# A graph layer and an FFN on one core: the first two FFN units spread over the last two neighbour sums, and ten bias adds moved behind the adjacency

## The chip, the cores and the metric

One core of a Trainium2 chip. The metric is the device time of one execution in microseconds; the median of three runs of the kernel before is 371.93. The engines are named as in the profile: PE is TensorE's matmuls and PEld its weight loads, DVE is VectorE, ACT is ScalarE, POOL is GpSimd, SP is SyncE, which issues the DMAs.

## The reference

x has 1250 nodes (rows) of 512 features; src and dst are 20000 edges, sorted by dst.

```python
def _L0_gnn_ref(x, src, dst, W_self, W_neigh, b):
    msg_sum = jax.ops.segment_sum(x[src], dst, num_segments=N_NODES)
    deg = jax.ops.segment_sum(jnp.ones((src.shape[0],), x.dtype), dst, num_segments=N_NODES)
    neigh = msg_sum / jnp.maximum(deg, 1.0)[:, None]
    h = x @ W_self + neigh @ W_neigh + b
    h = jnp.where(h >= 0, h, LEAKY_SLOPE * h)
    norm = jnp.sqrt(jnp.sum(h * h, axis=1, keepdims=True))
    return h / jnp.maximum(norm, EPS)
def _quantize_weight(w, group_size):
    o, i = w.shape
    wg = w.reshape(o, i // group_size, group_size)
    scale = jnp.mean(jnp.abs(wg), axis=-1, keepdims=True) + EPS
    wq = jnp.clip(jnp.round(wg / scale), -1.0, 1.0) * scale
    return wq.reshape(o, i)
...
gate = _bitlinear(x, w_gate)
up = _bitlinear(x, w_up)
h = jax.nn.silu(gate) * up
return _bitlinear(h, w_down)
...
x = x + _L0_gnn_ref(_layernorm(x, axis=-1), src, dst, L0_gnn_W_self, L0_gnn_W_neigh, L0_gnn_b)
x = x + _L0_ffn_ref(_layernorm(x, axis=-1)[None], L0_ffn_w_gate, L0_ffn_w_up, L0_ffn_w_down)[0]
```

The FFN is 512 to 1408 and back; a group of the quantiser is 128 inputs, so each 128x128 block of a weight is a ternary block (-1, 0, 1) times one scale for each of its output rows.

## The kernel before, in words

The kernel is written engine by engine. Each engine runs its list of instructions in order; semaphores tie the lists together, and an instruction that waits holds up all that is behind it on its engine. Nodes come in ten tiles of 125 (t = 0 to 9), features in four blocks of 128.

**First stage.** 80 slots, eight for each tile. In them TensorE multiplies tile t's normalised rows with W_neigh (y, kept as a high and a low part, `y_hi` and `y_lo`) and with W_self (z), and in between builds the adjacency `a_t` from one-hot rows: VectorE makes `hot_dst` (L904) and `hot_src` (L900), ScalarE copies finished blocks of 40 nodes out (`block_out`, L682). Beside that the 34 weight loads of the FFN are made ternary, a load being up to four 128x128 blocks: ScalarE takes absolute values and their sums (`abs_of`, L642), GpSimd makes of a load's sums a threshold `thr` (L561) and the scales `nscale` (L562), and VectorE compares (`ternary_of`, L841), which waits for both. Two loads can be in ScalarE's absolute values at a time, four in `raw`. 25 loads are done in this stage, and nine of the down weights (33 blocks; called load 0 to 8 here) later. GpSimd also adds the bias to each z tile, in the slots:

```python
for slot in range(SLOTS + 8):
    t, i = divmod(slot, 8)
    for j in jobs_in(slot, 7):
        ... scales_of(l)
    if i == 4 and 1 <= t <= NT:
        ...
        pool.wait_ge(z_out, t)
        nc.gpsimd.tensor_tensor(z[:, t - 1, :], z[:, t - 1, :], bias_b[0:TP, :], ALU.add).then_inc(z_done, 1)
for l in range(LOADS1, len(loads)):
    scales_of(l)
```

**Neighbour sums.** Sum n (n = 0 to 9) is 20 matmuls on TensorE (L1127) into banks 4 and 5 in turn. Then, for tile n: VectorE `neighbour_sum` (L925, from PSUM into z), `leak` (L931), ScalarE square and root (L727, L729), VectorE `residual` (L937 to L948: x_sb and its layer-norm statistics), ScalarE's root (L691), VectorE `shift1` (L953, L955), ScalarE `normalize1` (L697, into one of two buffers `xn`), TensorE's transpose (L1039), ScalarE `x1_high` (L704) and VectorE `x1_low` (L960). Sum n+2 waits for `neighbour_sum(n)`. In program order the steps of tiles trail: `residual(n - 1)` in turn n of VectorE, `normalize1(n - 2)` on ScalarE, the transpose of tile n-3 after sum n on TensorE. The ternary blocks of loads 0 to 8 are spread over turns 1 to 6.

**FFN.** 33 units (f, c): f is one of 11 blocks of 128 of the 1408, c one of three groups of tiles (0 to 2, 3 to 5, 6 to 9; 378, 378 and 504 columns). A unit has eight gate and up pieces (G0, U0, G1, ... U3), each two matmuls into one of seven banks; ScalarE takes G0 and U0 out of PSUM (L748), VectorE the other six (L997), accumulating with the scale of the block. Then ScalarE's SiLU (L770), GpSimd h = silu times up (L595), ScalarE `h_hi` (L787), GpSimd `h_lo` (L604). Three units later come four down pieces D1, D2, D3, D0; ScalarE takes D1 and D3 into `d_one` and GpSimd adds them to `acc` (L585), VectorE takes the others. Ternary blocks go through bank 7: transposed on TensorE (L1110, L1114), out with a sign on ScalarE (L714, L717). Units 0 to 5 are (0,0), (0,1), (1,0), (1,1), (0,2), (1,2). When a tile group is complete, output pieces (O) transpose `acc` (L1174), and the tile is added to x_sb by VectorE (L1031), or by ScalarE and GpSimd (L802, L612), and stored. A turn n of the FFN is the gate and up pieces of unit n with the down pieces of unit n-3.

## Time and profile before

| | |
|---|---|
| median of 3 runs | 371.93 us (371.62 to 371.94) |
| the profiled execution | 372.08 us, its span 370.1 us |
| PE busy | 340.7 us, 92% of the span |
| DVE busy | 312.9 us, 85% |
| ACT busy | 235.4 us, 64% |
| POOL busy | 173.8 us, 47% |
| mean granted TensorE clock | 0.989 |

How to read it: TensorE is the busiest engine, but a share of the whole span hides that the stages differ. The busy time of TensorE is modelled from the ends of pipelined matmuls; the distance between the starts of two matmuls tells more than their durations. In the timelines the first number is the start in us from the span's start, the second the us that it lasted, and brackets at the end hold how long the engine was idle before, and who released it.

### The profile page before, as it was taken

The page shows a single profiled execution, that of the slowest core. Times are in us where ns is not written, and L with a number is a line of the kernel's source. Part 1 is how long each engine was busy: PE and PEld are TensorE (multiplying, and loading weights), DVE is VectorE, ACT ScalarE, POOL GpSimd, SP SyncE. Part 2 cuts the span into 40 slices and gives each one's busy share as a digit, 9 for nine tenths or more (in the row PEclk, how much of TensorE's full clock was granted, in tenths as well). Part 3 has the DMA queues.
Part 4 walks back from the last instruction along what each step waited for, and adds up shares of the span by engine and source line. Part 5 has one row for each costly group of instructions (what it writes and reads, how often), then busy time and mean ns, then how long its engine had stood idle before and what let it go on. Part 6 is the DMA issues. An engine that isn't in the chain of part 4 may idle for free.

```text
span 370.1 us, 5903 instructions
## 1 busy us (share of the span) xinstructions
PE 340.7 (92%) x1741; PEld 260.3 (70%) x1741; DVE 312.9 (85%) x746; ACT 235.4 (64%) x637; POOL 173.8 (47%) x218
## 2 busy tenths in 40 slices
PE   2988999999999999999866999999999999999992
PEld 1444555555555667778655888889899898889981
DVE  2599999898898517999688799999999988999994
ACT  2174877777768224775556777777676678776660
POOL 3003343342122210111003456788788887799990
PEclk9999999999999999999989999999999999999997
DMA  7951222322212101200000000000000000000214
GB/s 229 291 143 45 71 83 60 86 58 70 74 50 81 31 1 30 75 25 0 3 0 2 0 1 2 0 3 1 0 3 0 2 2 2 0 0 3 90 34 156
DMA packets 9412, 16.70 MB, mean 45 GB/s; under 512 B 1062, under 2 KB 1886, under 8 KB 9378
## 3 DMA queue, kind: packets, MB, share of 16 engines
q1 hardware_dynamic: 9300, 16.21, 15.4%
q8 instruction: 15, 0.25, 0.3%
q14 instruction: 19, 0.16, 0.1%
q10 hardware_dynamic: 78, 0.08, 0.1%
HBM read 13.73 MB, written 2.56 MB: 44 GB/s over the span
## 4 chain that ended last, share of the span: by engine, by line
PE 63%; DVE 23%; ACT 7%; POOL 3%; issue 2%; POOLq 0%; DVEq 0%; ACTq 0%
PE bank L1198 39%; PE bank L1087 9%; PE bank L1127 5%; DVE hot_dst L904 4%; DVE tq_gu L841 3%; PE bank L1048 3%; DVE tq_d L841 2%; ACT mag_early L642 2%; PE bank L464 2%; DVE bn L946 2%; DVE x_sb L943 1%; DVE bn L827 1%; PE bank L1039 1%; DVE z L925 1%; DVE hot_src L900 1%
## 5 line engine op out<-in xcount | busy, mean ns | idle before, releaser
L1198 PE MATMUL bank<-x_hi,t_gu 128*128 128x378 f32 (+1 forms) x264 | 96.2, 364 | 3.6 <-DVE x_lo L960 2.8
L1198 PE MATMUL bank<-x_lo,t_gu 128*128 128x378 f32 (+1 forms) x264 | 94.7, 359 | 0.0
L1087 PE MATMUL bank<-w_sb,xnT 128*125 128x512 f32 x160 | 87.6, 635 | 2.2 <-ACT z L672 1.5
L997 DVE SCALAR_TENSOR_TENSOR g_acc<-bank,nscale,g_acc 128x378 f32<-128x378 f32 (+1 forms) x99 | 64.3, 650 | 11.9 <-PE bank L1198 11.3
L561 POOL TENSOR_SCALAR thr<-absum 128x4 f32<-128x4 f32 (+1 forms) x34 | 15.8, 464 | 112.2 <-ACT mag_early L642 79.5
L997 DVE SCALAR_TENSOR_TENSOR u_acc<-bank,nscale,u_acc 128x378 f32<-128x378 f32 (+1 forms) x99 | 64.1, 647 | 0.6 <-PE bank L1198 0.6
L595 POOL TENSOR_TENSOR hh<-sg,u_acc 128x378 f32<-128x378 f32 (+1 forms) x32 | 35.1, 1097 | 57.6 <-ACT sg L770 57.4
L1048 PEld LDWEIGHTS bank<-hot_dst,hot_src 128*125 128x125 bf16 x281 | 32.2, 137 | 39.9 <-issue 22.2
L585 POOL TENSOR_TENSOR acc<-acc,d_one 128x378 f32<-128x378 f32 (+1 forms) x57 | 60.1, 1055 | 0.0
L1198 PEld LDWEIGHTS bank<-x_hi,t_gu 128*128 128x128 f32 x264 | 50.4, 191 | 8.1 <-DVE x_lo L960 3.5
L1198 PEld LDWEIGHTS bank<-x_lo,t_gu 128*128 128x128 f32 x264 | 50.6, 192 | 3.6
L904 DVE TENSOR_SCALAR hot_dst<-iota,key 128x400 bf16<-128x400 uint16 x157 | 47.4, 340 | 4.7 <-PE bank L1048 4.3
L1198 PE MATMUL bank<-h_hi,t_d 128*128 128x378 f32 (+1 forms) x132 | 48.1, 364 | 0.0
L1198 PE MATMUL bank<-h_lo,t_d 128*128 128x378 f32 (+1 forms) x132 | 46.6, 353 | 0.0
L642 ACT ACTIVATE mag_early<-raw 128x128 f32<-128x128 f32 x99 | 29.6, 301 | 23.9 <-DVE tq_gu L841 22.3
L1048 PE MATMUL bank<-hot_dst,hot_src 128*125 128x240 bf16 (+4 forms) x281 | 40.4, 264 | 3.0 <-DVE hot_dst L904 3.0
L997 DVE SCALAR_TENSOR_TENSOR acc<-bank,nscale,acc 128x378 f32<-128x378 f32 (+1 forms) x63 | 40.1, 645 | 1.0 <-POOL acc L585 1.0
L1127 PE MATMUL bank<-y_hi,a_t 125*125 125x512 f32 x100 | 40.1, 401 | 0.0
L1127 PE MATMUL bank<-y_lo,a_t 125*125 125x512 f32 x100 | 39.5, 395 | 0.0
L604 POOL TENSOR_TENSOR h_lo<-hh,h_hi 128x378 fp32r<-128x378 f32 (+1 forms) x32 | 35.0, 1095 | 3.4 <-ACT h_hi L787 1.9
L748 ACT ACTIVATE d_one<-bank,nscale 128x378 f32<-128x378 f32 (+1 forms) x57 | 34.8, 610 | 2.1 <-PE bank L1198 1.9
L748 ACT ACTIVATE g_acc<-bank,nscale 128x378 f32<-128x378 f32 (+1 forms) x33 | 20.2, 612 | 24.3 <-PE bank L1198 24.3
(107 smaller groups left out, 549.4 us busy)
## 6 DMA issues: line engine op xcount, KB each, us to landing
raw<-in_L_ffn_w_gate SPq DMA_DIRECT2D x11, 256.0 KB, 2.7
raw<-in_L_ffn_w_up SPq DMA_DIRECT2D x11, 256.0 KB, 2.6
out_x<-x_sb SPq DMA_DIRECT2D x10, 224.0 KB
raw<-in_L_ffn_w_down SPq DMA_DIRECT2D x8, 256.0 KB, 2.6
x_sb<-in_x SPq DMA_DIRECT2D x1, 1344.0 KB
w_sb<-in_L_gnn_W_neigh SPq DMA_DIRECT2D x1, 1024.0 KB, 6.2
w_sb<-in_L_gnn_W_self SPq DMA_DIRECT2D x1, 1024.0 KB, 7.1
raw<-in_L_ffn_w_down SPq DMA_DIRECT2D x4, 192.0 KB, 2.3
```

Source lines behind the costliest of these rows:

```text
L585: nc.gpsimd.tensor_tensor(to, to, d_one[:, o, slot, 0:width(u)], ALU.add).then_inc(d_added, 1)
L595: nc.gpsimd.tensor_tensor(hh[:, u % 2, 0:w], sg[:, u % 2, 0:w], u_acc[:, u % 2, 0:w], ALU.mult).then_inc(h_done, 1)
L604: nc.gpsimd.tensor_tensor(h_lo[:, u % h_slots, 0:w], hh[:, u % 2, 0:w], h_hi[:, u % h_slots, 0:w].bitcast(F32), ALU.subtract).then_inc(hlo ...
L642: nc.scalar.activation(mag_of(j), raw_of(j), ACT.Abs, accum_out=absum[:, j:j + 1]).then_inc(abs_done, 1)
L748: nc.scalar.activation(to, bank_of(u, what)[:, 0:width(u)], ACT.Copy, scale=nscale[:, j:j + 1]).then_inc(act_took, 1)
L841: nc.vector.scalar_tensor_tensor(out=tq_of(j), in0=mag_of(j), scalar=thr[:, j:j + 1], in1=raw_of(j), op0=ALU.is_gt, op1=ALU.mult).then_inc ...
L904: nc.vector.tensor_scalar(hot_dst[:, c % HOT, :], iota[:, 0:NT * WIN], key[:, c:c + 1], None, ALU.is_equal).then_inc(hot_made, 1)
L997: nc.vector.scalar_tensor_tensor(out=to, in0=bank_of(u, what)[:, 0:w], scalar=nscale[:, j:j + 1], in1=to, op0=ALU.mult, op1=ALU.add).then_ ...
L1048: last = nc.tensor.matmul(bank[k % 3][0:TP, 0:NT * WIN].rearrange("p (s d) -> p s d", d=WIN)[:, :, d0:d0 + n], hot_src[:, c // SB % SBS, c ...
L1087: last = nc.tensor.matmul(to[0:TP, :], xnT[:, t, k * TP:(k + 1) * TP], w_sb[:, k, half * D:(half + 1) * D], start=k == 0, stop=k == KD - 1)
L1127: last = nc.tensor.matmul(bank[4 + n % 2][0:TP, :], a_t[:, s, n * TP:(n + 1) * TP], y[:, s, :], start=s == 0 and y is y_hi, stop=s == NT - ...
L1198: last = nc.tensor.matmul(to, w, parts[h], start=h == 0, stop=h == 1)
```

## The change

Units 1 and 2 change places. The pieces of units 0 and 1 are issued between the matmuls of sums 8 and 9 (`EARLY_AT`: one piece after each of the steps 1 to 8 of a sum), over banks 2 and 6. The nine late loads are done in VectorE's turns up to 3 (`DOWN`). A tile's steps trail its sum by less: residual in its own turn, the transpose after sum t+2. GpSimd's bias adds come after `block_out`, and one instruction makes all scales at the end. The down pieces of units 0 and 1 come in turn 5, those of 2 and 3 in turn 6, and the order is as before from turn 7 on. g_acc and u_acc have four buffers, h has five slots, and the FFN's buffers lie at other addresses. D3 of unit 31 goes to ScalarE and GpSimd, and the outputs of tiles 0 to 2 come one turn later.

```diff
-    h_slots = 4
+    h_slots = 5
+        DOWN = [0, 3, 5, 7, 8, NL]
         def down_jobs(n):
-            lo, hi = (LOADS1 + max(0, min(NL, 3 * i // 2)) for i in (n, n + 1))
+            lo, hi = (LOADS1 + DOWN[min(max(i, 0), len(DOWN) - 1)] for i in (n + 1, n + 2))
-        UNITS = [(0, 0), (0, 1), (1, 0), (1, 1), (0, 2), (1, 2)]
+        UNITS = [(0, 0), (1, 0), (0, 1), (1, 1), (0, 2), (1, 2)]
-            return what in ("G0", "U0") or what in ("D1", "D3")[:max(0, min(2, NU - 1 - u))]
+            return what in ("G0", "U0") or what in ("D1", "D3")[:2 if u < NU - 1 else 0]
+        EARLY = 2
+        EARLY_AT = [1, 2, 3, 4, 5, 6, 7, 8]
+            downs[{0: 5, 1: 5, 2: 6, 3: 6}.get(u, u + LAG)].append(u)
-                if n == (u + LAG + 1 if u < NU - 3 else NU + LAG - 1):
+                if n == {FINAL[0]: FINAL[0] + LAG + 1, FINAL[1]: NU + LAG - 2, FINAL[2]: NU + LAG - 1}[u]:
-        RING = [2, 6, 1, 0, 4, 3, 5]
+        RING = [2, 6] * (4 * EARLY) + [2, 6, 4, 5, 3] * 4
+        RING += [[2, 6, 4, 5, 3, 0, 1][i % 7] for i in range(len(pieces) - len(RING))]
...
# GpSimd
+            for l in range(LOADS1):
                 scales_of(l)
+            pool.wait_ge(bias_in, 16)
+            pool.wait_ge(block_out, NB)
+            for t in range(NT):
+                pool.wait_ge(z_out, t + 1)
+                nc.gpsimd.tensor_tensor(z[:, t, :], z[:, t, :], bias_b[0:TP, :], ALU.add).then_inc(z_done, 1)
+                if 1 <= t <= NL:
+                    scales_of(LOADS1 + t - 1)
+
+            nc.gpsimd.tensor_scalar(nscale[:], absum[:], 1.0 / P, Q_EPS, ALU.mult, ALU.add).then_inc(nscales, 1)
...
# VectorE
+            for j in down_jobs(-1):
+                ternary_of(j)
+            for n in range(NT):
+                neighbour_sum(n)
+                leak(n)
+                if n >= 1:
+                    shift1(n - 1)
+                if n >= 2:
+                    x1_low(n - 2)
+                u = n - NT + 3
+                if u >= 0:
+                    take(u, "G1")
+                    if u < EARLY:
+                        take(u, "U1")
+                residual(n)
+                if 0 <= u < EARLY:
+                    for what in ("G2", "U2", "G3", "U3"):
+                        take(u, what)
+                for j in down_jobs(n):
+                    ternary_of(j)
...
# TensorE
+                    if s == NT - 1:
+                        last.then_inc(n_ready, 1)
+                    if u >= 0 and s in EARLY_AT:
+                        piece(8 * u + EARLY_AT.index(s))
...
+                if n >= 2:
+                    transpose_x1(n - 2)
```

GpSimd's list from the last load of the first stage to down load 1 (thr is the threshold, z the bias add), before:

```order
L561 TENSOR_SCALAR thr<-absum 128x4 [waits abs_done]
L562 TENSOR_SCALAR nscale<-absum 128x4
L574 TENSOR_TENSOR z<-z,bias_b 125x512 [waits z_out] x2
L561 TENSOR_SCALAR thr<-absum 128x4 [waits abs_done]
L562 TENSOR_SCALAR nscale<-absum 128x4
L561 TENSOR_SCALAR thr<-absum 128x3 [waits abs_done]
L562 TENSOR_SCALAR nscale<-absum 128x3
```

and with the change:

```order
L590 TENSOR_SCALAR thr<-absum 128x4 [waits abs_done]
L598 TENSOR_TENSOR z<-z,bias_b 125x512 [waits z_out,block_out,bias_in]
L598 TENSOR_TENSOR z<-z,bias_b 125x512 [waits z_out]
L590 TENSOR_SCALAR thr<-absum 128x4 [waits abs_done]
L598 TENSOR_TENSOR z<-z,bias_b 125x512 [waits z_out]
L590 TENSOR_SCALAR thr<-absum 128x3 [waits abs_done]
L598 TENSOR_TENSOR z<-z,bias_b 125x512 [waits z_out]
```

All ten adds have moved behind the last adjacency block, and from the third on each stands between two thresholds.

VectorE's list from the degrees to sum 1 (tq_d is a ternary block, z from a bank the sum, z from z the leak), before:

```order
L916 RECIPROCAL rdeg<-rs 125x6 [waits rdeg_done]
L925 SCALAR_TENSOR_TENSOR z<-bank,rdeg,z 125x512 [waits z_done,n_ready,rdeg_done]
L931 SCALAR_TENSOR_TENSOR z<-z 125x512 [waits hsum]
L925 SCALAR_TENSOR_TENSOR z<-bank,rdeg,z 125x512 [waits z_done,n_ready]
L937 TENSOR_SCALAR nrm<-nrm 125x1 [waits norms]
```

and with the change:

```order
L959 RECIPROCAL rdeg<-rs 125x6 [waits rdeg_done]
L884 SCALAR_TENSOR_TENSOR tq_d<-mag_late,thr,raw 128x128 [waits scales,rdeg_done]
L884 SCALAR_TENSOR_TENSOR tq_d<-mag_late,thr,raw 128x128 [waits scales] x10
L968 SCALAR_TENSOR_TENSOR z<-bank,rdeg,z 125x512 [waits z_done,n_ready]
L974 SCALAR_TENSOR_TENSOR z<-z 125x512 [waits hsum]
L980 TENSOR_SCALAR nrm<-nrm 125x1 [waits norms]
L982 RECIPROCAL inv<-nrm 125x1 [waits inv_done]
L984 SCALAR_TENSOR_TENSOR x_sb<-z,inv,x_sb 125x512 [waits inv_done]
L987 BN_STATS bn<-x_sb 125x6 [waits x1_done]
L989 BN_AGGR mv_118<-bn 125x2 [waits bn_done]
L884 SCALAR_TENSOR_TENSOR tq_d<-mag_late,thr,raw 128x128 [waits scales] x8
L968 SCALAR_TENSOR_TENSOR z<-bank,rdeg,z 125x512 [waits z_done,n_ready]
```

Eleven ternary blocks now stand ahead of sum 0 and eight ahead of sum 1, and the residual of tile 0 is in its own turn.

ScalarE's list from the first SiLU to unit 4's first take (sg is the SiLU, g_acc from a bank a take; only unit 4 has 504 columns here), before:

```order
L770 ACT_TABLE_LOAD
L770 ACTIVATE sg<-g_acc 128x378
L787 ACTIVATE h_hi<-hh 128x378
L714 ACTIVATE t_gu<-bank 128x1024
L704 ACTIVATE x_hi<-bank 128x504
L748 ACTIVATE g_acc<-bank,nscale 128x378
L748 ACTIVATE u_acc<-bank,nscale 128x378
...
L717 ACTIVATE t_d<-bank 128x512
L748 ACTIVATE g_acc<-bank,nscale 128x504
```

and with the change:

```order
L731 ACTIVATE x_hi<-bank 128x504
L800 ACT_TABLE_LOAD
L800 ACTIVATE sg_78<-g_acc_70 128x378
L800 ACTIVATE sg_79<-g_acc_71 128x378
L806 ACTIVATE h_hi<-hh_80 128x378
L806 ACTIVATE h_hi<-hh_81 128x378
L800 ACTIVATE sg_78<-g_acc_72 128x378
L746 ACTIVATE t_d_90<-bank 128x512
L806 ACTIVATE h_hi<-hh_80 128x378
L762 ACTIVATE g_acc_70<-bank,nscale 128x504
```

The SiLU and h_hi steps of units 0 to 2, which stood between takes, now stand together behind the last tile's x_hi and ahead of unit 4's first take.

## Rows read from the trace of the kernel before

**Rows 1.** Windows: stretch, us, busy PE, PEld, DVE, ACT, POOL (count), clock, DMA share, GB/s.
```profile
185.00:195.00 10.00, 6.18 (x29) 5.47 (x30) 8.63 (x21) 5.57 (x12) 0.00 (x0) 0.83 0.00 0
195.00:205.00 10.00, 6.39 (x45) 5.45 (x43) 7.64 (x15) 6.32 (x11) 3.94 (x4) 1.00 0.01 2
215.00:300.00 85.00, 85.00 (x487) 76.97 (x486) 79.51 (x139) 61.94 (x115) 68.44 (x66) 1.00 0.01 1
```

**Rows 2.** Waits of TensorE from 10 to 127 us.
```profile
PE bank L1087 <- ACT z L672: 1.5, 4, 0.6
```

**Rows 3.** Timeline of TensorE: start us, us, line, operation [idle before <-releaser].
```profile
155.57 0.65 PE L1039 MATMUL bank<-ident,xn 126*128 126x126 f32 x4 [0.73 <-ACT xn L697]
166.24 0.48 PE L1127 MATMUL bank<-y_hi,a_t 125*125 125x512 f32 x1
171.31 0.47 PE L1127 MATMUL bank<-y_hi,a_t 125*125 125x512 f32 x1
182.02 0.40 PE L1127 MATMUL bank<-y_lo,a_t 125*125 125x512 f32 x1
204.74 0.42 PE L1198 MATMUL bank<-x_hi,t_gu 128*128 128x378 f32 x1
224.73 0.34 PE L1198 MATMUL bank<-x_hi,t_gu 128*128 128x378 f32 x1
```

**Rows 4.** Chain that ended last: start us, us, what.
```profile
188.00 3.48 PE bank L1198 x10
204.98 3.84 PE bank L1198 x22
```

**Rows 5.** Timelines of GpSimd and VectorE near 43 us.
```profile
43.00 1.27 POOL L574 TENSOR_TENSOR z<-z,bias_b 125x512 f32<-125x512 f32 x1
43.08 1.61 DVE L841 SCALAR_TENSOR_TENSOR tq_gu<-mag_early,thr,raw 128x128 bf16<-128x128 f32 x2
46.05 0.60 DVE L841 SCALAR_TENSOR_TENSOR tq_gu<-mag_early,thr,raw 128x128 bf16<-128x128 f32 x2
```

**Rows 6.** Timelines of ScalarE and VectorE in the sums.
```profile
127.58 0.65 ACT L682 ACTIVATE a_t<-bank 125x400 fp32r<-125x400 f32 x2 [1.67 <-PE bank L1048]
132.59 0.75 DVE L925 SCALAR_TENSOR_TENSOR z<-bank,rdeg,z 125x512 f32<-125x512 f32 x1 [5.66 <-PE bank L1127]
134.86 0.20 ACT L729 ACTIVATE nrm<-ss 125x1 f32<-125x1 f32 x1
139.42 0.75 DVE L925 SCALAR_TENSOR_TENSOR z<-bank,rdeg,z 125x512 f32<-125x512 f32 x1 [5.35 <-PE bank L1127]
154.17 1.13 DVE L841 SCALAR_TENSOR_TENSOR tq_d<-mag_late,thr,raw 128x128 bf16<-128x128 f32 x4
155.22 0.74 DVE L925 SCALAR_TENSOR_TENSOR z<-bank,rdeg,z 125x512 f32<-125x512 f32 x1
192.03 0.14 DVE L937 TENSOR_SCALAR nrm<-nrm 125x1 f32<-125x1 f32 x1
193.92 0.18 DVE L948 BATCH_NORM_AGGREGATE mv<-bn 125x2 f32<-125x6 f32 x1
```

**Rows 7.** Timelines of ScalarE and GpSimd at the first SiLU.
```profile
194.45 1.28 ACT L770 ACT_TABLE_LOAD   x1
196.35 0.99 POOL L595 TENSOR_TENSOR hh<-sg,u_acc 128x378 f32<-128x378 f32 x1 [27.50 <-ACT sg L770]
197.97 0.98 POOL L604 TENSOR_TENSOR h_lo<-hh,h_hi 128x378 fp32r<-128x378 f32 x1 [0.63 <-ACT h_hi L787]
```

**Rows 8.** Timelines of VectorE, GpSimd, TensorE in the tail.
```profile
357.74 0.60 DVE L997 SCALAR_TENSOR_TENSOR acc<-bank,nscale,acc 128x378 f32<-128x378 f32 x1
358.39 2.55 POOL L612 TENSOR_TENSOR x_sb<-x_sb,d_one 125x512 f32<-125x512 f32 x2
361.85 2.17 DVE L997 SCALAR_TENSOR_TENSOR acc<-bank,nscale,acc 128x378 f32<-128x378 f32 x4 [0.98 <-POOL acc L585]
364.17 1.76 PE L1174 MATMUL bank<-ident,acc 128*125 128x128 f32 x12 [2.90 <-DVE acc L997]
```

More of the change, by code:

```diff
@@ L403, in bank_of @@
         def bank_of(u, what):
-            return bank[RING[index[u, what] % len(RING)]]
+            return bank[RING[index[u, what]]]
         def nodes_of(u):
@@ new lines, in _, with silu, high_of_h @@
+            ternary_out(0, 1)
+            normalize1(NT - 1)
+            take(3, "G0", g_of(3))
+            take(3, "U0", u_of(3))
+            x1_high(NT - 1)
+            def silu(u):
+                act.wait_ge(dve_took, took[u, "G3"])
+                if u >= 2:
+                    act.wait_ge(h_done, u - 1)
+                nc.scalar.activation(sg_of(u), g_of(u), ACT.Silu).then_inc(silu_done, 1)
+            def high_of_h(u):
+                act.wait_ge(h_done, u + 1)
+                if u >= h_slots:
+                    act.wait_ge(piece_ready, index[u - h_slots, "D0"] + 1)
+                nc.scalar.activation(h_hi[:, u % h_slots, 0:width(u)], hh_of(u), ACT.Copy).then_inc(hhi_done, 1)
@@ L771, in _ @@
                 for what in ("D1", "D2", "D3"):
-                    v = n - LAG
-                    if 0 <= v and by_act(v, what):
-                        o = int(what[1])
+                    for v in downs[n]:
+                        if not by_act(v, what):
+                            continue
                         if (v, what) not in added:
-                            take(v, what, acc[:, o, nodes_of(v)])
+                            take(v, what, acc[:, int(what[1]), nodes_of(v)])
@@ L1005, in low_of_h @@
                                         ALU.subtract).then_inc(hlo_done, 1)
-            for n in range(NU + LAG):
+            for n in range(EARLY, NU + LAG):
                 for what in TURN:
-                    u = n - LAG if what[0] == "D" else n
-                    if 0 <= u < NU and not by_act(u, what):
-                        take(u, what)
+                    for u in units_of(n, what):
+                        if not by_act(u, what) and (u, what) != (EARLY, "G1"):
+                            take(u, what)
+                    if n == 2 and what == "U1":
+                        shift1(NT - 1)
+                    if n == 2 and what == "U2":
+                        x1_low(NT - 2)
                     if n == 3 and what == "U1":
-                        x1_low(9)
+                        x1_low(NT - 1)
                     if n == NU - 1 and what == "U3":
@@ new lines, in transpose_x1, with output_piece @@
+            def transpose_x1(t):
+                if t >= 2:
+                    pe.wait_ge(xlo_done, t - 1)
+                transpose_xn(t, normed1, x1_bank(t), x1n_T, TQ)
+            def output_piece(t):
+                v = out_of[t]
+                pe.wait_ge(dve_took, took[v, "D0"])
+                for o in range(1, KD):
+                    if by_act(v, f"D{o}"):
+                        pe.wait_ge(d_added, added[v, f"D{o}"])
+                for k in range(KD):
+                    last = nc.tensor.transpose(bank_of(t, "O")[0:TP, k * P:(k + 1) * P], acc[:, k, t * TQ:t * TQ + TP], ident[:])
+                last.then_inc(piece_ready, 1)
@@ L1161, in _, with piece @@
+            def piece(i):
+                u, what = pieces[i]
+                if bank_before[i] is not None:
+                    old = pieces[bank_before[i]]
                     pe.wait_ge(took_sem(*old), took[old])
                 else:
[L1164 to L1165 removed]
+                    pe.wait_ge(*{2: (block_out, NB), 6: (z_out, NT), 4: (hsum, NT - 1), 5: (hsum, NT), 3: (squares, NT),
+                                 0: (xlo_done, NT - 1), 1: (xlo_done, NT)}[RING[i]])
@@ L1166, in _ @@
                 if what == "O":
-                    v = out_of[u]
-                    pe.wait_ge(dve_took, took[v, "D0"])
-                    for o in range(1, KD):
-                        if by_act(v, f"D{o}"):
-                            pe.wait_ge(d_added, added[v, f"D{o}"])
-                    for k in range(KD):
-                        last = nc.tensor.transpose(bank_of(u, what)[0:TP, k * P:(k + 1) * P], acc[:, k, u * TQ:u * TQ + TP], ident[:])
-                    last.then_inc(piece_ready, 1)
```

314 lines of the change are left out of this document (144 added, 170 removed).

## The prediction

> **What bounds the kernel now.** I read a table of stretches first, then the waits, the timeline of TensorE, and then the places where engines hand over to each other. The stretches [rows 1] show an FFN stage in which TensorE is busy all the time (85 of 85 us), and just ahead of it two poor stretches (6.2 and 6.4 us busy of 10, from 185 to 205 us). In the first stage (projections and adjacency, to 127.4 us) TensorE waits 1.5 us in all for ScalarE's z [rows 2]; its other wait there, for the first hot rows, the change does not touch. In the sums TensorE waits 0.73 us at 155.57 for a normalised tile; the last sum is out at 182.42, and the even run of FFN pieces starts at 204.74 [rows 3]. Of these 22.3 us the 48 matmuls of units 0 to 2 fill 8.4, at 3.84 us for 22 [rows 4], and the transposes 2.7, so it waits some 11. Part of it runs slow: ten matmuls take 3.48 us there, not 1.75 [rows 4], at a granted clock that averages 0.83 [rows 1], so partly at 1.2 GHz. From 204.74 on TensorE is the bound.
>
> **What the change moves.** (a) 32 matmuls (units 0 and 1) go from that gap into sums 8 and 9. (b) GpSimd's ten bias adds on z leave the first stage; they start when the last adjacency block is out, and alternate with the thresholds of the down weights. (c) All 33 down ternaries on VectorE stand in front of sum 4's work. (d) Tile t's transpose stands after sum t+2 on TensorE, was after t+3. (e) ScalarE's first SiLU steps stand behind tile 9 and ahead of unit 4's takes. (f) The output pieces of tiles 0 to 2 stand one turn later.
>
> **First stage: -1.0 us.** A bias add takes 1.27 us. One starts at 43.00, and the two ternaries that VectorE begins at 43.08 take 1.61 us together, where two take 0.60 otherwise [rows 5]. So such an add on GpSimd keeps an instruction of this kind off for about 1.0 us. With the change that leaves VectorE's first stage, but TensorE sees of it only the 1.5 us for ScalarE's z, whose queue holds absolute values that wait for VectorE's ternaries. Between 0 and 1.5 I take 1.0, since the lateness grows step by step behind these ternaries.
>
> **Early sums: +9.3 us.** This term decides. I keep the clock of the trace of before. The last block is out at 128.23 [rows 6]. GpSimd then adds bias 0 and 1 (to 130.8), makes threshold 0 (131.1) and at once starts bias 2: as at 43.00, the add is ahead of the ternary that waited for its scale. From then on each of the down loads 0 to 7 pays a hold of 1.0 us [rows 5], and four ternaries 1.05 (154.17 to 155.22 [rows 6]), three 0.8. Loads 0 to 2 come ahead of sum 0 on VectorE: with the thresholds, and ScalarE's absolute values of load 2 that can start only when load 0 is ternary, VectorE is free at 137.1; before, it took sum 0 up at 132.59.
> One turn of VectorE costs 4.5 us without ternaries: 2.45 from taking up a sum to ScalarE's root (132.59 to 135.06), and 2.1 for the residual and statistics (192.03 to 194.10) [rows 6]; the shift and x_lo of other tiles fit below ScalarE's part. So VectorE takes up sum 1 at 137.1 + 4.5 + 2 x 2.05 = 145.7, sum 2 at 145.7 + 4.5 + 1.8 + 2.05 = 154.05, sum 3 at 154.05 + 4.5 + 2.05 + 0.4 (degrees) = 161.0, and sum 4 at 161.0 + 4.5 + 0.8 = 166.3. Before, it took up sum 1 at 139.42 and sum 4 at 155.22 [rows 6].
> Tile t-1 is normalised 2.45 + 0.8 = 3.25 us after VectorE takes up sum t: tile 0 at 148.95, tile 1 at 157.3, tile 2 at 164.25. TensorE has ended sum 2 at 144.9 and stands, in order, at tile 0's transpose: a wait of 4.05. A sum and a transpose cost 5.07 (166.24 to 171.31 [rows 3]), 4.63 of it the sum. Sum 3 ends at 154.0, wait 3.3; sum 4 at 162.35, wait 1.9; sum 5 ends at 169.75, and tile 3 is there at 169.55. The waits sum to 9.25. Behind each waiting transpose stand all later sums; the waits in turn give VectorE time, so it is not late any more at sum 7.
> The bounds: with no hold at all the same chain gives waits of 0.15, 1.3 and 0.9, together 2.4; with a hold for the whole 1.27 it gives 11.4. I take the 1.0 of the row, which is the same pair of instructions.
>
> By the Trainium skill, "SBUF — State Buffer", section Who interferes with whom, VectorE and GpSimd have one pair of ports in common: a VectorE instruction with two SBUF inputs and a GpSimd instruction that reads SBUF exclude each other, and the later one waits for all of the other. The pair at 43.08 shows the exclusion, but 1.0 us of it. By the page the early sums would cost 11.4 us, and the sum below would be 380.9.
>
> **From sum 8 to unit 7: -0.7 us.** Without these waits sum 8 would start at 171.31 - 0.73 + 0.43 (one more transpose) + 1.1 (three weight transposes) = 172.1. Sums 8 and 9 hold eight pieces each (16 matmuls, 2.8 us) over only two banks. VectorE takes piece G2 behind the residual, so G3 gets its bank 7.05 us into the sum, not 5.8: sum 8 lasts 8.67, the transpose 0.43, sum 9 is out after 8.85, at 190.05. Call this R; before, R was 182.42 [rows 3].
> After R: root +2.5; residual and statistics behind one take +5.0; ScalarE's root +5.35; shift behind another take +5.8; tile 9 normalised +6.65. Its transpose stands behind piece U1 of unit 3, whose bank VectorE frees at +7.95, so x_hi of tile 9 is out at +9.7. Then table load and SiLU, 1.9 to GpSimd's h (194.45 to 196.35), and GpSimd and ScalarE hand over to each other: from h to h_lo 1.62, h_lo 0.98 [rows 7]. Unit 4's first take on ScalarE stands behind h_hi of unit 2, so this passes twice, 5.2, and then h, h_hi and the take of G0, 2.1. That is +18.9, and +19.1 with VectorE 0.2 late. TensorE has five pieces of unit 4 done at +12.8 and stands 6.3 us at the sixth for G0's bank. To unit 7 it is then the 20.0 us of before (204.74 to 224.73 [rows 3]) less unit 3 (2.8), its weight transpose (0.2) and five wide pieces (2.3), plus 0.2 of slow takes: 14.9. Unit 7 starts at 190.05 + 19.1 + 14.9 = 224.05, before at 224.73. The gap is not filled: most of it comes again behind other instructions.
>
> **Clock: +1.0 us.** Before, ten matmuls took 1.7 us too long after two waits of together 2.8 us [rows 4]. After one of 6.3 I expect the same; part of it lies under the takes. Bounds 0 and 1.7.
>
> **Tail: -1.9 us.** Before, two output adds on GpSimd (358.39 to 360.94) stand ahead of its last accumulation; VectorE waits 0.98 us for that at 361.85, and the last transposes start at 364.17 [rows 8]. Now the accumulations stand ahead, and one more of them is GpSimd's. VectorE: D0 of unit 30 ends at 358.3 [rows 8], two takes 359.3, an output add 360.0, four takes 362.1; transposes at 362.2. TensorE is through with its pieces near 360.1 (28 matmuls and transposes from 355.9) and covers none of it. Bounds 0 (the added accumulation of 1.0 ends last) and -2.4.
>
> **Sum.** The profiled execution took 372.08 us, 0.15 above the median of 371.93. 372.08 + 9.3 - 0.7 + 1.0 - 1.0 - 1.9 = 378.8. The layout, the single scale instruction and the fifth h slot I cost at nothing: GpSimd has nothing to do between the last threshold and unit 0's SiLU, which covers the 132-column scale; were it late, the first take in sum 8 would be late by as much, under 1 us.
>
> **Rivals.** *The holds cost nothing in the sums (chance 0.10).* For it: the same adds ran beside a full VectorE in the first stage, and TensorE lost next to nothing. Against: there the hot rows are made ahead; here TensorE waits in order for what VectorE makes. Waits of 2.4 instead of 9.3: 371.9.
> *TensorE never waits at the early transposes (0.22), faster.* For it: VectorE was idle 5.66 and 5.35 us before it took up sums 0 and 1 [rows 6], which would hold the 8.7 us of ternaries, if the adds fall in other gaps and ScalarE has its absolute values early. Against: the add comes right after the threshold each time. 378.8 - 9.3 = 369.5. It decides from 2.6 us of waits: with less than that the change wins.
> *The clock falls at each early wait too (0.13), slower.* Against: TensorE is ahead of VectorE there, so a slow sum is hidden. Three times 1.7 on top, less what is hidden: up to 383.5.
> *My forecast (0.55): 378.8*, its own range 376.5 to 381.5 (tail 0, clock 0 or 1.7, hold 1.27).
>
> **Numbers.** Range 369.0 to 382.5: it leaves out about half of the faster case and most of the slowest. 0.2% (0.74 us) is about what a measurement of this kernel can tell from no change. Slower 0.55 + 0.13 = 0.68; same 0.10; faster 0.22.
>
> **What would show it.** In the changed trace: down ternaries with maxima near 1.3 us between 131 and 160; TensorE idle for 3 to 4 us before the tile transposes after sums 2 and 3, released by ScalarE's xn; sum 8 starting near 180.4; an idle of 6 us some 13 us after the last sum, released by ScalarE's take; unit 7 near 232. I am wrong if GpSimd's adds are through before VectorE wants its thresholds, or if ScalarE's takes of unit 4 come before h of unit 2.

## The result and the profile after

The changed kernel takes 383.09 us (median of four executions, 382.71 to 384.0), the kernel before 371.94 beside it (371.62 to 372.07): 1.030 times as long, 95% interval 1.028 to 1.032. The forecast was 378.8 with a range to 382.5, so the direction was right and the size too small. The profiled execution took 382.97 us, of which the span is 380.9; before it was 372.08 and 370.1. Every comparison of places below is made inside these spans.

The waits of TensorE from 127 to 230 us, in the changed kernel (line, what it waited for, us in total, times, longest):

```profile
PE bank L1086 <- ACT xn L724: 10.2, 4, 4.9
PE bank L1218 <- ACT g_acc L762: 5.6, 1, 5.6
PE bank L1218 <- DVE g_acc L1023: 2.2, 2, 1.1
```

Its timeline of TensorE, as in [rows 3]; L1236 is a neighbour sum, L1086 a tile's transpose, L1218 a piece of the FFN, L1182 the last transposes:

```profile
125.75 0.51 PE L1236 MATMUL bank<-y_hi,a_t 125*125 125x512 f32 x1
...
148.40 1.10 PE L1086 MATMUL bank<-ident,xn 126*128 126x126 f32 x4 [4.91 <-ACT xn L724]
...
156.84 0.65 PE L1086 MATMUL bank<-ident,xn 126*128 126x126 f32 x4 [1.14 <-ACT xn L724]
...
164.19 0.62 PE L1086 MATMUL bank<-ident,xn 126*128 126x126 f32 x4 [2.07 <-ACT xn L724]
...
199.06 0.40 PE L1236 MATMUL bank<-y_lo,a_t 125*125 125x512 f32 x1
...
218.84 0.79 PE L1218 MATMUL bank<-x_hi,t_gu 128*128 128x504 f32 x1 [5.62 <-ACT g_acc L762]
219.43 0.62 PE L1218 MATMUL bank<-x_lo,t_gu 128*128 128x504 f32 x1
...
236.33 0.34 PE L1218 MATMUL bank<-x_hi,t_gu 128*128 128x378 f32 x1
...
373.95 1.55 PE L1182 MATMUL bank<-ident,acc 128*125 128x128 f32 x12 [1.64 <-DVE acc L1023]
```

Both groups of waits that were forecast are there: three at the early transposes, and one of 5.6 us before a piece of unit 4, which ends when ScalarE takes G0 out. Sum 9 ends at 199.3, so that one begins 13.9 us later. The table of stretches, with the columns of [rows 1] (PE and PEld busy, VectorE, ScalarE, GpSimd, then the granted clock), shows one thing that was priced too low:

```profile
127.00:155.00 28.00, 23.09 (x96) 17.11 (x95) 22.27 (x44) 11.61 (x64) 12.64 (x16) 0.88 0.15 43
...
205.00:215.00 10.00, 8.12 (x39) 6.24 (x37) 6.72 (x13) 5.40 (x9) 2.80 (x3) 0.88 0.00 0
215.00:225.00 10.00, 6.16 (x22) 4.93 (x23) 3.99 (x6) 5.18 (x10) 5.02 (x6) 0.66 0.00 0
```

From 215 to 225 us the granted clock averages 0.66, so most of that stretch ran at 1.2 GHz, and the wide matmuls from 218.84 on stand 0.42 us apart, where they stand 0.23 apart at the full clock.

The timeline of GpSimd where the down weights begin (POOL L598 is the bias add, L590 the threshold, DVE L884 the ternary, ACT L669 the absolute value):

```profile
126.69 2.56 POOL L598 TENSOR_TENSOR z<-z,bias_b 125x512 f32<-125x512 f32 x2 [12.46 <-issue]
129.33 0.20 POOL L590 TENSOR_SCALAR thr<-absum 128x4 f32<-128x4 f32 x1
129.61 1.30 POOL L598 TENSOR_TENSOR z<-z,bias_b 125x512 f32<-125x512 f32 x1
131.00 0.20 POOL L590 TENSOR_SCALAR thr<-absum 128x3 f32<-128x3 f32 x1
131.27 1.30 POOL L598 TENSOR_TENSOR z<-z,bias_b 125x512 f32<-125x512 f32 x1
```

The timeline of VectorE beside it (L968 takes up sum 0):

```profile
129.63 1.43 DVE L884 SCALAR_TENSOR_TENSOR tq_d<-mag_late,thr,raw 128x128 bf16<-128x128 f32 x1 [4.38 <-POOL thr L590]
131.25 1.47 DVE L884 SCALAR_TENSOR_TENSOR tq_d<-mag_late,thr,raw 128x128 bf16<-128x128 f32 x1
...
136.88 0.74 DVE L968 SCALAR_TENSOR_TENSOR z<-bank,rdeg,z 125x512 f32<-125x512 f32 x1
...
149.67 4.03 DVE L884 SCALAR_TENSOR_TENSOR tq_d<-mag_late,thr,raw 128x128 bf16<-128x128 f32 x7
158.27 2.28 DVE L884 SCALAR_TENSOR_TENSOR tq_d<-mag_late,thr,raw 128x128 bf16<-128x128 f32 x4
165.38 0.87 DVE L884 SCALAR_TENSOR_TENSOR tq_d<-mag_late,thr,raw 128x128 bf16<-128x128 f32 x3
```

And ScalarE's first absolute value of load 2:

```profile
133.07 0.31 ACT L669 ACTIVATE mag_late<-raw 128x128 f32<-128x128 f32 x1 [4.01 <-DVE tq_d L884]
```

A ternary takes 0.34 us, and three in a row 0.87 (165.38, where no add is left). The one that begins with the add at 129.61 ends 0.15 us behind it, after 1.43, and the one at 131.25 again ends 0.15 behind an add. By the Trainium skill, "SBUF — State Buffer", section Who interferes with whom, the later of two such instructions waits for all of the other. The trace agrees that it does not end before the other is through; the loss is 1.1 us (1.43 less 0.34) beside an add of 1.30. The 1.0 us that I took from [rows 5] was a little short for one pair, not for the mean over all loads.

In the first stage, TensorE's waits for ScalarE's z fall from the 1.5 us of [rows 2] to 0.8. Its first matmul on hot rows, the kernel before above the changed one:

```profile
21.62 0.85 PE L1048 MATMUL bank<-hot_dst,hot_src 128*125 128x240 bf16 x3 [1.36 <-DVE hot_dst L904]
```

```profile
21.16 0.85 PE L1095 MATMUL bank<-hot_dst,hot_src 128*125 128x240 bf16 x3 [1.36 <-DVE hot_dst L947]
```

From there to the start of sum 0 it is 105.81 us before (to 127.43) and 104.59 with the change (to 125.75).

### The profile page after: what moved, and what is told of

It reads as the page before. It is cut to its first block, busy times and chain, and to the rows that moved or that the text cites. A ratio compares the mean times of both kernels' runs of the same rounds, so it can differ in the third digit from the quotient of the medians.

```text
span 380.9 us, 5900 instructions
## 1 busy us (share of the span) xinstructions
PE 344.7 (90%) x1741; PEld 263.6 (69%) x1741; DVE 316.1 (83%) x745; ACT 236.3 (62%) x638; POOL 160.4 (42%) x186
## 4 chain that ended last, share of the span: by engine, by line
PE 67%; DVE 17%; issue 6%; ACT 5%; POOL 3%; DVEq 0%; ACTq 0%; POOLq 0%
PE bank L1218 37%; PE bank L1134 13%; PE bank L1236 5%; PE bank L1095 4%; DVE tq_d L884 4%; DVE hot_dst L947 2%; PE bank L1086 2%; PE bank L1157 1%; DVE bn L870 1%; DVE tq_gu L884 1%; PE bank L1182 1%; ACT bank L753 1%; DVE z L968 1%; DVE z L974 1%; DVE acc L1023 1%
## 5 line engine op out<-in xcount | busy, mean ns | idle before, releaser
L1218 PE MATMUL bank<-x_hi,t_gu 128*128 128x378 f32 (+1 forms) x264 | 97.4, 369 | 7.9 <-ACT g_acc L762 5.6
L1218 PE MATMUL bank<-x_lo,t_gu 128*128 128x378 f32 (+1 forms) x264 | 96.0, 364 | 0.0
L590 POOL TENSOR_SCALAR thr<-absum 128x4 f32<-128x4 f32 (+1 forms) x34 | 11.2, 329 | 123.9 <-ACT mag_early L669 100.6
L1218 PEld LDWEIGHTS bank<-x_hi,t_gu 128*128 128x128 f32 x264 | 51.1, 194 | 14.8 <-ACT g_acc L762 6.1
L611 POOL TENSOR_TENSOR acc<-acc,d_one 128x378 f32<-128x378 f32 (+1 forms) x58 | 61.1, 1057 | 0.0
L947 DVE TENSOR_SCALAR hot_dst<-iota,key 128x400 bf16<-128x400 uint16 x157 | 44.6, 319 | 11.8 <-PE bank L1095 11.2
L1218 PEld LDWEIGHTS bank<-x_lo,t_gu 128*128 128x128 f32 x264 | 51.1, 194 | 4.3
L1218 PE MATMUL bank<-h_hi,t_d 128*128 128x378 f32 (+1 forms) x132 | 48.5, 368 | 0.2
L1218 PE MATMUL bank<-h_lo,t_d 128*128 128x378 f32 (+1 forms) x132 | 46.7, 354 | 0.0
L669 ACT ACTIVATE mag_early<-raw 128x128 f32<-128x128 f32 x99 | 29.6, 301 | 21.0 <-DVE tq_gu L884 19.8
L1236 PE MATMUL bank<-y_hi,a_t 125*125 125x512 f32 x100 | 41.3, 413 | 0.0
L1236 PE MATMUL bank<-y_lo,a_t 125*125 125x512 f32 x100 | 40.4, 404 | 0.0
L762 ACT ACTIVATE g_acc<-bank,nscale 128x378 f32<-128x378 f32 (+1 forms) x33 | 20.2, 613 | 30.7 <-PE bank L1218 30.6
```

Source lines behind the costliest of these rows:

```text
L611: nc.gpsimd.tensor_tensor(to, to, d_one[o][slot][:, 0:width(u)], ALU.add).then_inc(d_added, 1)
L669: nc.scalar.activation(mag_of(j), raw_of(j), ACT.Abs, accum_out=absum[:, j:j + 1]).then_inc(abs_done, 1)
L762: nc.scalar.activation(to, bank_of(u, what)[:, 0:width(u)], ACT.Copy, scale=nscale[:, j:j + 1]).then_inc(act_took, 1)
L947: nc.vector.tensor_scalar(hot_dst[:, c % HOT, :], iota[:, 0:NT * WIN], key[:, c:c + 1], None, ALU.is_equal).then_inc(hot_made, 1)
L1218: last = nc.tensor.matmul(to, w, parts[h], start=h == 0, stop=h == 1)
L1236: last = nc.tensor.matmul(bank[4 + n % 2][0:TP, :], a_t[:, s, n * TP:(n + 1) * TP], y[:, s, :], start=s == 0 and y is y_hi, stop=s == NT - ...
```

## The experiments

The profiled executions begin their sums at 124.8 to 127.4 us, also where the first stage is the same. So I compare places by the time since the first matmul of sum 0. The scatter lies ahead of the first matmul on hot rows, which starts between 20.2 and 21.8 us; these are the rows that the adjacency is built from. From there to sum 0 it is 105.8 us in the kernel before and e4, 104.9 in e1, e3, e6, e7 and e9, and 104.6 in the changed kernel, e2, e5, e8, e10 and e11, each time within 0.03 us. All medians are on a chip beside the kernel before (372.0 in each of the three sets of experiments). "Ladder" names the fuller reorder of ScalarE's list in e5.

| kernel | median us | sum 0 starts | sum 8, after sum 0 | end of sum 9 | last transposes | end, after those |
|---|---|---|---|---|---|---|
| before | 371.94 | 127.43 | 43.88 | 54.6 | 236.74 | 5.93 |
| changed | 383.09 | 125.75 | 55.29 | 73.3 | 248.20 | 6.95 |
| e1 adds back | 373.98 | 126.72 | 46.38 | 64.4 | 238.38 | 6.80 |
| e2 takes ahead | 379.81 | 125.39 | 55.28 | 73.3 | 245.55 | 6.86 |
| e3 both | 371.17 | 125.41 | 46.41 | 64.4 | 235.10 | 7.99 |
| e4 tail alone | 370.67 | 126.90 | 43.88 | 54.6 | 234.84 | 6.76 |
| e5 ladder | 375.81 | 126.34 | 55.28 | 73.3 | 241.14 | 6.92 |
| e6 ladder, adds back | 366.73 | 125.93 | 46.41 | 64.4 | 231.68 | 7.99 |
| e7 as e6, O turn | 368.12 | 126.25 | 46.36 | 64.4 | 233.60 | 5.95 |
| e8 adds moved alone | 374.14 | 125.57 | 47.19 | 58.0 | 240.81 | 6.02 |
| e9 as e6, spread | 369.24 | 125.65 | 46.89 | 64.9 | 232.72 | 6.83 |
| e10 half adds | 375.26 | 124.77 | 49.65 | 67.7 | 241.23 | 6.80 |
| e11 spread, adds moved | 381.03 | 125.95 | 54.59 | 72.6 | 246.03 | 6.72 |

(Places from the timelines of TensorE; the end of sum 9 is the start of its last matmul, the last column the span less the start of the last transposes.)

**e1: the bias adds back in the first stage.**

```diff
-            for l in range(LOADS1):
-                scales_of(l)
-            pool.wait_ge(bias_in, 16)
-            pool.wait_ge(block_out, NB)
-            for t in range(NT):
-                ... add bias to tile t, scales_of(LOADS1 + t - 1)
+            for slot in range(SLOTS + 8):
+                ... scales of the slot's jobs; add bias to tile t - 1 if i == 4
+            for l in range(LOADS1, len(loads)):
+                scales_of(l)
```

> The changed kernel with GpSimd's ten bias adds back in the slots of the first stage, as in the kernel before; the ternaries in front, the transposes two sums behind and the rest stay. Theory 1 (the early sums are late because each bias add keeps one down ternary of VectorE off for 1.1 to 1.2 us): no ternary after 127 us lasts over 0.4 us, the first sum starts 1.7 us later (127.4, was 125.75), the waits before the transposes after sums 2, 3 and 4 (8.1 us) and the slow sum 3 (2.2 us) shrink to 0 to 2.4 us, sum 8 starts at 172 to 174.5 (was 181.05), and the time is 374 to 377. Theory 2 (the order does it: eight ternaries and more ahead of sum 0's work, and transposes one sum earlier than before, adds or no adds): the waits stay at 6 us or more and the time stays at 380 or above, or gets worse by the 1.7 us of the first stage.

Measured: 373.98 us, ratio to before 1.004 (1.001 to 1.006), 9.1 less than the changed kernel. The ternaries after 127 us in one row (min, median, max in ns):

```profile
L888 DVE SCALAR_TENSOR_TENSOR tq_d<-mag_late,thr,raw x33: 321/347/354, 129.8 to 158.0; 128x128 bf16<-128x128 f32 x33
```

And in TensorE's timeline the waits that are left, before the transposes after sums 3 and 4:

```profile
150.04 0.65 PE L1090 MATMUL bank<-ident,xn 126*128 126x126 f32 x4 [0.51 <-ACT xn L728]
156.25 0.62 PE L1090 MATMUL bank<-ident,xn 126*128 126x126 f32 x4 [0.93 <-ACT xn L728]
```

No ternary is long, and sum 8 comes 8.9 us earlier after sum 0. Theory 1 holds. Its 1.7 us for the first stage was wrong: from the first hot rows to sum 0 the adds cost 0.3 us here (104.92 for 104.59).

**e2: unit 4's and unit 5's takes ahead in ScalarE's list.** The lines with "..." stand for waits on semaphores and for loop conditions.

```diff
...
                 if n == 1:
                     silu(0)
                     silu(1)
+                    ...
+                    take(4, "G0", g_of(4))
                 elif n == 2:
                     high_of_h(0)
+                    take(4, "U0", u_of(4))
                 elif n == 3:
+                    silu(2)
                     high_of_h(1)
-                    silu(2)
+                    ternary_out(1, 1)
+                    ...
+                    take(5, "G0", g_of(5))
+                    silu(3)
+                    ...
+                    take(5, "U0", u_of(5))
+                    high_of_h(2)
...
```

> The changed kernel with ScalarE's list reordered after tile 9: the takes of G0 and U0 of unit 4 stand behind SiLU 1 and h_hi of unit 0, ahead of h_hi of units 1 and 2; unit 5's stand ahead of h_hi of unit 2. Theory 1 (TensorE's 5.6 us at 213.2 are the place of these takes in ScalarE's order, and the slow 2.5 us behind them are the clock after that idle): TensorE goes through unit 4 at 213 with less than 1 us idle, the slow stretch from 218.8 to 224.2 is gone, up to 2 us come again at the first down pieces, and the time is 375.5 to 378.5. Rival (the ladder of h, h_hi and h_lo bounds this place, wherever the takes stand): the idle moves to the down pieces of units 0 and 1 and the clock falls there, the time is 381 to 383.

Measured: 379.81 us, 3.3 less than the changed kernel, between the two expectations. The 5.6 us are gone, but others stand behind them:

```profile
215.91 0.62 PE L1167 MATMUL bank<-ident_b,tq_gu 128*128 128x128 bf16 x8 [1.30 <-ACT t_d L746]
...
222.82 0.50 PE L1228 MATMUL bank<-x_hi,t_gu 128*128 128x504 f32 x1 [2.53 <-ACT acc L762]
```

Both are released by ScalarE: the first by the sign of weight block (1,1), which I had put behind a step that waits for GpSimd, the second by the take of D1, which stands behind h_hi of unit 3. So it is again the order of its list, one turn later.

**e3: both edits.** The diffs of e1 and e2 together.

> Both edits together: bias adds in the first stage, and the takes of units 4 and 5 ahead. If both terms are what I say and do not lean on each other, the gains add: 366.5 to 371, so about 2 us faster than the kernel before in the middle. If they share a cause (a late VectorE gives the clock or the ladder a better start), the sum of the two gains is missed by over 1.5 us.

Measured: 371.17 us, ratio 0.997 (0.994 to 0.999), 11.9 below the changed kernel, where the two gains make 12.4. The terms add within 0.5 us, though the executions of e3 lie 5.2 us apart (368.44 to 373.63). The range I gave ended at 371, which took e2's gain larger than it was.

**e4: the tail's edits in the kernel before.**

```diff
-            return what in ("G0", "U0") or what in ("D1", "D3")[:max(0, min(2, NU - 1 - u))]
+            return what in ("G0", "U0") or what in ("D1", "D3")[:2 if u < NU - 1 else 0]
...
-                if n == (u + LAG + 1 if u < NU - 3 else NU + LAG - 1):
+                if n == {FINAL[0]: FINAL[0] + LAG + 1, FINAL[1]: NU + LAG - 2, FINAL[2]: NU + LAG - 1}[u]:
```

> The kernel before with the edits of the tail alone: D3 of unit 31 is taken by ScalarE and added by GpSimd, and the output pieces of tiles 0 to 2 stand one turn later. Theory 1: the last transposes start 1.8 us earlier (362.4, was 364.17), as in the changed kernel from unit 7 on, but the stores of two tile groups now run together, so that the span ends 6.9 us behind the start of these transposes and not 5.9: the time is 0.8 us lower, 371.1. Rival 1 (the 1.0 us of the last stores was chance): 1.8 lower, 370.1. Rival 2 (the added accumulation on GpSimd ends last here): no change.

Measured: 370.67 us, ratio 0.996 (0.994 to 0.998), 1.35 less than before. The last transposes start 1.9 us earlier after sum 0, and the span ends 6.76 us after them, not 5.93. Theory 1 holds: 1.9 less 0.8. The DMA lines, 8 us in 40 slices, show what goes on in the stores, first in the kernel before from 363 us on, then in the changed one from 373 us on:

```profile
DMA  6953200000000000079999997666764100000000
```

The changed kernel:

```profile
DMA  0003999612999768896688997899999621100000
```

Before, the stores of the second last tile group are through by 364 us and those of the last have the queues alone. Now they run into each other: six stores of 224 KB are issued in the changed kernel's last 8 us, as in e4 from 361 us on, where the kernel before has three.

**e5: the rest of ScalarE's list.** Against e2 the sign of (1,1) stands ahead of unit 3's takes, and behind unit 5's take of U0 the list reads

```diff
...
+                    take_down(0, "D1")
+                    high_of_h(2)
+                    take_down(1, "D1")
+                    silu(4)
+                    ternary_out(2, 0)
+                    high_of_h(3)
+                    take_down(0, "D3")
+                    take_down(1, "D3")
+                    high_of_h(4)
...
```

> The changed kernel (bias adds moved) with a fuller reorder of ScalarE's list than in the second run: the sign of block (1,1) out of bank 7 stands ahead of unit 3's takes, and the first down pieces D1 and D3 of units 0 and 1 are taken ahead of h_hi of units 3 and 4. Theory (what was left there was again the place of takes in the list: 1.3 us before L1167 for t_d, 2.5 us before a piece for ScalarE's acc, and the slow clock behind it): both idles fall below 0.6 us in all, no matmul between 205 and 235 us is slow, and the time is 376 to 377.5, from 379.8. Rival (the ladder h, h_hi, h_lo at 2.6 us a unit bounds the down pieces): TensorE waits 2 us or more for h_lo, time 379 or above.

Measured: 375.81 us, 7.3 less than the changed kernel. The time is 0.2 us below the range. Between 205 and 235 us TensorE has two idles left, of 0.18 and 0.28 us. The theory holds for the waits; the hand-over of h between GpSimd and ScalarE does not bound this place. That no matmul there would be slow did not come true: behind an idle of 2.04 us at 203.92 they run at half the clock from 204.7 to 208.1.

**e6: the same with the bias adds in the first stage.** The diffs of e1 and e5.

> The same reorder, with the bias adds in the slots of the first stage. If the terms add: 371.2 less 3.0 to 4.0, so 367 to 368.5, which is faster than both kernels. The early waits stay at 1.4 us, the last sum is out 64.5 us after the first began.

Measured: 366.73 us, ratio to before 0.985 (0.982 to 0.987): faster than both kernels, and a little below the range. The stretches that answer to the three above:

```profile
127.00:155.00 28.00, 27.02 (x123) 19.99 (x121) 21.97 (x65) 16.81 (x82) 3.05 (x9) 1.00 0.15 43
...
205.00:215.00 10.00, 9.83 (x55) 8.34 (x53) 8.94 (x15) 7.18 (x14) 7.87 (x8) 1.00 0.00 1
215.00:225.00 10.00, 9.65 (x58) 8.38 (x58) 9.01 (x18) 7.70 (x15) 8.41 (x9) 1.00 0.01 2
```

TensorE is busy and the clock is full in all three. The reorder is worth 7.3 us both ways (e1 less e6, and the changed kernel less e5).

**e7: the output pieces one turn earlier, in e6.** It takes the second half of e4's diff back.

> As the run before, with the output pieces of tiles 0 to 2 one turn earlier, as in the kernel before; D3 of unit 31 stays with ScalarE and GpSimd. Theory (two things fight in the tail: GpSimd's output adds ahead of its last accumulations delay the last transposes, and output adds behind them push six stores together): the last transposes start 1.5 to 2.8 us later against the first sum, the end comes 5.9 us after them and not 6.8 to 8, so the time is 0.3 to 2 us worse than in the run before. Rival (the stores are what ends last): 0.5 us or more better.

Measured: 368.12 us, 1.4 more than e6. The last transposes start 1.9 us later and the end follows after 5.95 us instead of 7.99. In the profiled executions the two cancel; in the medians the earlier transposes win. The later turn alone moves the transposes by 1.9 us here, as both edits together did in e4, so D3 of unit 31 adds nothing that shows; in the stores the turn costs 0.8 to 2.0.

**e8: only the bias adds moved, in the kernel before.** Its POOL list gets the loop of the change.

> The kernel before with nothing but the ten bias adds moved behind the last adjacency block, between the thresholds, as in the change. Its ternaries are spread over turns 1 to 6 and its transposes stand three sums behind. Theory 1 (the holds cost time only where little slack stands between VectorE and a transpose): ternaries of up to 1.5 us show after 128 us as in the changed kernel, but the sums before sum 8 wait under 3 us in all (0.7 in the kernel before), and the time is 371 to 374.5. Theory 2 (the hold of each add costs by itself, in any order): 8 holds of 1.16 us show nearly whole, 378 or above.

Measured: 374.14 us, ratio 1.006 (1.004 to 1.008). The longest ternary takes 1.43 us, and sum 8 starts 3.3 us later than before; TensorE waits 0.82, 1.50 and 1.44 us before three transposes, 3.8 in all and not under 3. The time is as theory 1 had it. Two rows beside it show that the exclusion works both ways, and not for ternaries alone; this add began while VectorE was in the leak of a tile, which reads z twice:

```profile
144.26 0.67 DVE L927 SCALAR_TENSOR_TENSOR z<-z 125x512 f32<-125x512 f32 x1
144.29 1.79 POOL L570 TENSOR_TENSOR z<-z,bias_b 125x512 f32<-125x512 f32 x1
```

e1 and e8 with the two kernels make a square. Moving the adds costs 3.3 us up to sum 8 in the old order (43.88 to 47.19) and 8.9 in the new one (46.38 to 55.29). It saves 1.2 us ahead of sum 0 in the old order (105.81 to 104.58) and 0.3 in the new one (104.92 to 104.59).

**e9: e6 with the down loads spread.**

```diff
-        DOWN = [0, 3, 5, 7, 8, NL]
+        DOWN = [0, 2, 4, 6, 8, NL]
```

> The best kernel so far (bias adds in the first stage, the fuller reorder on ScalarE) with the down loads spread 2, 2, 2, 2, 1 over the turns of VectorE instead of 3, 2, 2, 1, 1. Theory (the 1.4 us that TensorE still waits at the transposes after sums 3 and 4 come of the ternaries ahead of tiles 1 and 2): the first waiting tile gets its turn 0.6 to 1.2 us earlier, but by tile 2's turn eight loads are done either way, so the waits fall by 0 to 1 us in all: 365.7 to 366.8. Rival (the later ternaries now delay tiles 3 and 4): waits of 2 us or more, 367.5 or above.

Measured: 369.24 us (366.44 to 370.95), ratio to before 0.991 (0.989 to 0.994). The time and the wait are the rival's, but not its place: the profiled execution has a single early wait, of 2.15 us instead of 0.5 and 0.9, at tile 2's transpose and not at those of tiles 3 and 4, and sum 8 at 46.89, half a microsecond later than e6. That does not make the 2.5 us between the medians. The executions fall into two groups: three of 366.4 to 367.3 us, the profiled one among them, with a mean granted clock of 0.992 to 0.993, and seven of 369.0 to 371.0 with 0.987 or 0.988. So what the median lost goes with a longer stretch at the lower clock; where in the kernel, no profile shows. No gain, in any case.

**e10: adds of half the width.**

```diff
-                nc.gpsimd.tensor_tensor(z[:, t, :], z[:, t, :], bias_b[0:TP, :], ALU.add)
+                nc.gpsimd.tensor_tensor(z[:, t, 0:256], z[:, t, 0:256], bias_b[0:TP, 0:256], ALU.add)
```

> The changed kernel with each of the ten moved bias adds cut to 256 of the 512 columns; the bias of the other columns is left out. It halves the dose. Theory (a ternary that meets an add is kept off until the add is through): the longest ternary is 0.85 to 1.0 us (1.5 with whole adds, 0.35 with none), sum 8 starts 50 to 52 us after sum 0 (55.3 with whole adds, 46.4 with none), and the time is 377 to 379.5. Rival (the order of GpSimd's list or the semaphores between the adds and the thresholds cost it, not the length of the add): sum 8 at 54 us or more, 381.5 or above.

Measured: 375.26 us, below the range; sum 8 at 49.65, a little below it too.

```profile
L884 DVE SCALAR_TENSOR_TENSOR tq_d<-mag_late,thr,raw x33: 339/340/927, 127.6 to 159.3; 128x128 bf16<-128x128 f32 x33
...
L598 POOL TENSOR_TENSOR z<-z,bias_b x9: 727/737/740, 126.4 to 152.3; 125x256 f32<-125x256 f32 x9
```

The longest ternary follows the length of the add (0.93 for 0.74, 1.50 for 1.30, 0.35 for none). With the adds cut from 1.29 to 0.74 us, 5.6 of the 8.9 us go, and two waits are left, of 0.99 and 1.99 us. The rival is out. The dose does not count in proportion: 43% less of each add takes away 63% of the cost. A reading of this that no run tests is that VectorE has some slack in these turns, and only the holds beyond it reach TensorE.

**e11: the changed kernel with the loads spread.** The diff of e9 on the changed kernel.

> The changed kernel, bias adds moved, with the down loads spread 2, 2, 2, 2, 1 instead of 3, 2, 2, 1, 1, and nothing else. Theory (VectorE's work and holds up to tile 2's turn bound the early sums, and eight loads lie ahead of it either way): the first wait falls from 4.9 us to 2 to 3.5, the later ones grow, sum 8 starts 54 to 55.5 us after sum 0, and the time is 381.5 to 383.5; a little may come back if the clock does not fall in sum 3. Rival (the three loads in front of sum 0 are the cause): sum 8 at 52 us or less, 379.5 or below.

Measured: 381.03 us. Sum 8 starts at 54.59, as the theory has it. The waits are 1.71, 3.46 and 1.51 us: the first fell below its range of 2 to 3.5, the second grew from 1.1, and the third did not grow. The time is 0.5 us below its range. Where the loads stand moves the waits about and does not remove them; what lies ahead of tile 2's turn on VectorE does.

## Why the prediction was too low

The mechanisms were the right ones, and most of the list of what would show it was found: ternaries of up to 1.5 us between 129.6 and 159, idles released by ScalarE's xn, sum 8 at 181.04 (forecast 180.4), an idle of 5.6 us (6.3) 13.9 us after the last sum, released by the take. Two places were off: the idles behind sums 2 and 3 were 4.9 and 1.1 us and not 3 to 4 each, and unit 7 starts at 236.3 and not near 232. Four terms were mis-sized. What follows is measured against 378.8, in which sum 0 starts at 127.43 as before, and in the profiled executions.

**Early sums, forecast +9.3, measured +10.6.** Sum 8 starts 55.29 us after sum 0; the chain without waits had 44.67. The hold was not the error: the 33 ternaries take 17.5 us, of which 9.6 are their own at 0.29 each, so eight holds cost 7.9, 1.0 each, as the row gave. The step that failed is "each of the loads pays a hold": the adds of bias 2 and of bias 3 both fell on the four ternaries of load 0, at 129.63 and 131.25, because threshold 1 was already to be had. ScalarE's absolute values of load 2 wait for the last of these four and start at 133.07, a hold late. VectorE took sum 0 up at 136.88, 11.1 us after its first matmul, forecast 9.7. From there all is 1.2 to 1.6 us late by the time since sum 0, up to sum 4 at 166.17. A hold for the whole add gave 11.4 us in the prediction; that this is nearer to 10.6 than my 9.3 is luck, since the mean hold was not that long. The clock fell in sum 3 as well (eight matmuls 0.43 us apart behind the 4.9 us wait), but the next wait was 1.1 us and not 3.3: as argued, a slow sum costs nothing where TensorE waits for VectorE behind it. VectorE took up sums 1 to 4 without a wait for TensorE. The rival in which it costs was wrong for that reason; the time came near its 383.5 by other terms.

**Clock, forecast +1.0, measured +2.5.** The matmuls after the idle of 5.6 us run at half the clock from 218.84 to 224.20. Ten wide ones and eight transposes of weights take 5.36 us; at the full clock they would take 2.9, by eight wide ones at 0.23, two at 0.31 (the first, and the one behind the transposes) and 0.43 for the transposes. "I expect the same" as after the 2.8 us of before failed: the slow stretch was longer, and no part of it lay under the takes. e5 takes the idle away, and these slow matmuls go with it, together 7.3 us.

**Tail, forecast -1.9, measured -0.8.** The transposes came as forecast: 137.62 us after unit 7's first piece, where 139.44 were needed before, 1.8 less. But I ended the tail at the transposes and let the last stores follow as before. That was the step that failed: the end came 1.0 us later after them, since moving an output piece also moves its store. e4 shows the same two terms alone, e7 takes both back.

**First stage, forecast -1.0, measured -1.2.** Sum 0 starts 1.7 us earlier. Of this 0.5 us lie ahead of the first hot rows, where kernels with the same first stage differ by as much and more. The other 1.2 us (105.81 to 104.59) are the change, and e8, in which only the adds moved, has them too. This term was right. In the changed kernel's order the adds account for 0.3 of it (e1); what gives the rest there was not run.

**From sum 8 to unit 7, forecast -0.7, measured about +0.2:** 0.5 us more in sums 8 and 9, 0.3 more to ScalarE's take, 0.1 behind it.

Together: +1.3 for the early sums, +1.5 for the clock, +1.1 for the tail, +0.9 from sum 8 to unit 7, and -0.7 ahead of sum 0 (-0.2 for the first stage, -0.5 for the scatter) is 4.1, and 378.8 + 4.1 is 382.9, the profiled 382.97. None of the misses is new in kind; all four go the same way, and the range had its upper end at the case of one mishap, not of four small ones.

The rival that had TensorE without waits, faster at 369.5, decided from 2.6 us of waits: there were 8.1 us. The rival in which holds are free would have had the waits of a kernel without holds. e1 is that kernel, with 1.4 us of them against the 2.4 of my lower bound.

## What to carry to other kernels

Before an instruction of GpSimd is moved out of a busy stage, look at what VectorE does at the new place and who waits in order behind it: the same ten adds cost 3.3 us where TensorE had a tile's slack and 8.9 us where it had not, and leaving the first stage they saved 1.2 and 0.3 us. When work is pulled ahead to fill a gap, follow the in-order list of the engine that hands over (here ScalarE) a turn further than the gap; with that list reordered (e5) and the adds left where they were, the same change gives 366.7 us instead of 383.1. And a tail ends with the last store: a piece moved towards the end takes its DMA with it.
